# Attention contexts on GpSimd taken three heads at a time, with the value columns reordered

## The reference, cut to what matters

```python
a = cumsum(poids); b = cumsum(poids * Z); result = a * Z - b      # along the sorted axis
context = result for poids = v - mean(v)
sum_relu = result for poids = 1
norm = maximum(2 * sum_relu - (Z * total_v - total_vz), 1e-4)
context = 2 * context / norm
x = x + context
```

## Time and profile before

| | |
|---|---|
| median of 3 runs | 1457.23 us (1455.3 to 1460.18) |
| profiled execution | 1457.44 us, its span 1456.1 us |
| busy in the span | PE 1106.8, PEld 905.9, DVE 947.5, ACT 825.8, POOL 607.7 us |
| sign tiles on ScalarE (L1274) | 224, 430.7 us busy |
| sign tiles on VectorE (L1448) | 288, 395.5 us busy |
| head matmuls (L1161) | 8192, 389.8 us busy |
| sums on VectorE (L1459) | 32, 59.1 us busy |
| contexts on GpSimd (L1488 to L1496) | 224 operations, 290.0 us busy |

### The profile page before, as it was taken

How to read it: one execution, slowest core, us unless ns; L and a number is a source line. 1 busy time by engine, 2 the same in 40 slices (tenths; PEclk the granted TensorE clock), 3 DMA queues, 4 the chain that set the end, 5 groups by cost and what they waited for, 6 DMA issues and landing times. The chain is left out here.

```text
span 1456.1 us, 30443 instructions
## 1 busy us (share of the span) xinstructions
PE 1106.8 (76%) x12280; PEld 905.9 (62%) x12280; DVE 947.5 (65%) x1573; ACT 825.8 (57%) x961; POOL 607.7 (42%) x599
## 2 busy tenths in 40 slices
PE   5355689888989899979898896374638965974698
PEld 2143575478888897648888883153317963642697
DVE  4212656799999965589999995223834645764365
ACT  6211444699999933389999986222613325653233
POOL 3744001026666640105666663754172430227244
PEclk9778699999999999999999998787868987987799
DMA  8867300412212100012121203275233333003343
GB/s 245 296 206 230 111 1 1 179 45 81 84 65 89 60 1 1 5 58 88 61 88 60 89 32 102 102 225 184 74 129 91 121 118 97 1 1 132 88 118 102
DMA packets 84588, 140.61 MB, mean 97 GB/s; under 512 B 10574, under 2 KB 71246, under 8 KB 79950
## 3 DMA queue, kind: packets, MB, share of 16 engines
q1 hardware_dynamic: 70276, 102.15, 21.9%
q0 software_dynamic: 13056, 35.87, 6.9%
q10 hardware_dynamic: 1120, 0.66, 0.2%
HBM read 86.62 MB, written 56.27 MB: 98 GB/s over the span
## 5 line engine op out<-in xcount | busy, mean ns | idle before, releaser
L1274 ACT ACTIVATE b_signs<-b_q_everywhere,normed 128x2048 bf16<-128x2048 f32 x224 | 430.7, 1991 | 27.4 <-PE banks L1161 26.6
L1161 PE MATMUL banks<-b_value_parts,b_signs 128*128 128x102 bf16 x8192 | 389.8, 208 | 47.5 <-DVE b_signs L1448 46.7
L1161 PEld LDWEIGHTS banks<-b_value_parts,b_signs 128*128 128x128 bf16 x8192 | 375.7, 97 | 64.4 <-DVE b_signs L1448 47.1
L1448 DVE TENSOR_SCALAR b_signs<-b_q_everywhere,normed 128x2048 bf16<-128x2048 f32 x288 | 395.5, 1434 | 5.8 <-PE banks L1161 5.8
L569 POOL DMA_INDIRECT moe_slots<-normed,slot_of_token x128 | 124.6, 973 | 39.3 <-issue 33.8
L1488 POOL TENSOR_TENSOR normed<-b_sums,normed 128x16 f32<-128x16 f32 x32 | 35.2, 1099 | 222.1 <-DVE b_sums L1459 222.1
L382 PE MATMUL banks<-identity,normed 128*128 128x128 f32 x256 | 49.8, 328 | 57.1 <-ACT normed L358 57.1
L331 DVE BATCH_NORM_STATS2 ln_stats<-residual 128x6 f32<-128x256 f32 x192 | 71.1, 417 | 22.3 <-SPq L1689 10.5
L382 PEld LDWEIGHTS banks<-identity,normed 128*128 128x128 f32 x256 | 32.4, 163 | 66.3 <-ACT normed L358 52.5
L1476 POOL MEMSET b_value_parts<- 128x256 bf16 x2 | 2.7, 1334 | 169.1 <-PE banks L1035 169.1
L391 PE MATMUL banks<-normed_T,wg 128*8 128x256 f32 x256 | 71.7, 406 | 0.0
(11 more groups left out here) (281 smaller groups left out, 2458.2 us busy)
## 6 DMA issues: line engine op xcount, KB each, us to landing
b_q_everywhere<-q_rows SPq DMA_DIRECT2D x32, 1024.0 KB, 4.7
normed<-expert_rows SPq DMA_DIRECT2D x6, 1024.0 KB, 10.3
d_rows<-moe_slots SPq DMA_DIRECT2D x40, 129.5 KB, 2.2
f_rows<-moe_slots SPq DMA_DIRECT2D x40, 129.5 KB, 2.3
moe_slots<-a_empty SPq DMA_DIRECT2D x8, 518.0 KB, 10.0
a_rows<-moe_slots SPq DMA_DIRECT2D x16, 259.0 KB, 4.2
moe_empty_slots<-a_empty SPq DMA_DIRECT2D x8, 518.0 KB, 5.6
moe_slots<-moe_empty_slots SPq DMA_DIRECT2D x1, 4144.0 KB
```

What stands on the lines that cost most here:

```text
L1161: ins = nc.tensor.matmul(banks[qt // QPB][:, qt % QPB * VP:(qt % QPB + 1) * VP], t.SG[:, (hh * TB + kt) % RING, qt * P:(qt + 1) * P], t.VO ...
L1274: nc.scalar.activation(t.SG[:, g % RING, :], t.QB[:, hh % 2, :], ACT.Sign, bias=t.NKT[:, kt, hh % H:hh % H + 1]).then_inc(s.sign_a, 1)
L1448: nc.vector.tensor_scalar(t.SG[:, g % RING, :], t.QB[:, hh % 2, :], t.KTM[:, kt, hh % H:hh % H + 1], 2.0, ALU.is_gt, ALU.mult).then_inc(s. ...
```

## The change

The six groups of heads of a batch are (0..2), (3..5), (6..8), (9..11), (12..14) and (15). `dve_sum` is still done once a head, now into one of two buffers of three heads. `pool_context` runs once a group, after the last sum of it, with four operations: q times the first 17 columns, minus the second 17, times the reciprocal of the norm, plus the residual. `dve_norm` runs once a group behind the sign tile kt = 14 of the head that follows the group, and does the clip as well as the reciprocal. The columns of a part are now value, one, value times k, k, so that norm and values stand in one operand of 17 columns each. The buffers of sums and contexts move into the place of the batch's transposed x.

```diff
+TOGETHER = ((0, 3), (3, 6), (6, 9), (9, 12), (12, 15), (15, 16))
+GH = 3
+def group_of(h):
+    return next(i for i, (lo, hi) in enumerate(TOGETHER) if lo <= h < hi)
...
 def value_columns(t, p, product, part):
-    at = part * VC + (DH if product else 0)
+    at = part * VC + (DH + 1 if product else 0)
...
 def pe_held(k, batch):
-    for tiles, lo, hi, ones in ((ACT_KT, 0, 2 * DH, k.ONESB), (DVE_KT, 2 * DH, VC, k.MINUSB)):
+    split = lambda ap, lo, hi: ap.rearrange("p h (m e) -> p h m e", e=DH + 1)[:, :, :, lo:hi]
+    for tiles, lo, hi, ones in ((ACT_KT, 0, DH, k.ONESB), (DVE_KT, DH, DH + 1, k.MINUSB)):
...
-                if h and kt == 14:
-                    dve_norm(k, hh - 1)
+                if kt == 14 and h in [hi for lo, hi in TOGETHER]:
+                    dve_norm(k, batch, group_of(h - 1))
...
 def dve_sum(k, hh):
     nc.vector.wait_ge(s.acc, TB * (hh + 1))
-    if hh >= 2:
-        nc.vector.wait_ge(s.ctx, hh - 1)
-    nc.vector.tensor_reduce(t.A[:, hh % 2, :, :].rearrange("p (b i) c -> p b i c", i=QPB), parts, AX_X, ALU.add).then_inc(s.sum, 1)
+    if h == TOGETHER[group][0] and g >= 2:
+        nc.vector.wait_ge(s.ctx, g - 1)
+    nc.vector.tensor_reduce(t.A[:, g % 2, h - TOGETHER[group][0], :, :].rearrange("p (b i) c -> p b i c", i=QPB), parts, AX_X,
+                            ALU.add).then_inc(s.sum, 1)
...
-def dve_norm(k, hh):
-    nc.vector.wait_ge(s.nf, hh + 1)
-    nc.vector.reciprocal(t.N1[:, r, :], t.N2[:, r, :]).then_inc(s.n2, 1)
+def dve_norm(k, batch, group):
+    nc.vector.wait_ge(s.nf, batch * len(TOGETHER) + group + 1)
+    k.vs.step(nc.vector.tensor_scalar(t.N[:, 0:n, :], t.CT[:, 0:n, :, DH], NORM_MIN, None, ALU.max))
+    nc.vector.reciprocal(t.N[:, 0:n, :], t.N[:, 0:n, :]).then_inc(s.n2, 1)
...
-def pool_context(k, batch, h):
-    nc.gpsimd.wait_ge(s.sum, hh + 1)
-    step(nc.gpsimd.tensor_tensor(t.N1[:, r, :], t.A[:, r, :, 2 * DH], q, ALU.mult))
-    step(nc.gpsimd.tensor_tensor(t.N2[:, r, :], t.N1[:, r, :], t.A[:, r, :, 2 * DH + 1], ALU.subtract))
-    nc.gpsimd.tensor_scalar(t.N2[:, r, :], t.N2[:, r, :], NORM_MIN, None, ALU.max).then_inc(s.nf, 1)
-    step(nc.gpsimd.tensor_tensor(t.CT, t.A[:, r, :, 0:DH], q.unsqueeze(2).broadcast_to([P, TB, DH]), ALU.mult))
-    step(nc.gpsimd.tensor_tensor(t.CT, t.CT, t.A[:, r, :, DH:2 * DH], ALU.subtract))
-    nc.gpsimd.wait_ge(s.n2, hh + 1)
-    step(nc.gpsimd.tensor_tensor(t.CT, t.CT, t.N1[:, r, :].unsqueeze(2).broadcast_to([P, TB, DH]), ALU.mult))
-    nc.gpsimd.tensor_tensor(x, x, t.CT, ALU.add).then_inc(s.ctx, 1)
+def pool_context(k, batch, group):
+    nc.gpsimd.wait_ge(s.sum, batch * H + hi)
+    step(nc.gpsimd.tensor_tensor(ct, total[:, :, :, 0:DH + 1], every(t.QTM[:, :, lo:hi].rearrange("p t h -> p h t"), DH + 1), ALU.mult))
+    nc.gpsimd.tensor_tensor(ct, ct, total[:, :, :, DH + 1:VC], ALU.subtract).then_inc(s.nf, 1)
+    nc.gpsimd.wait_ge(s.n2, g + 1)
+    step(nc.gpsimd.tensor_tensor(ct[:, :, :, 0:DH], ct[:, :, :, 0:DH], every(t.N[:, 0:n, :], DH), ALU.mult))
+    nc.gpsimd.tensor_tensor(x, x, ct[:, :, :, 0:DH], ALU.add).then_inc(s.ctx, 1)
```

More of the change, by code:

```diff
@@ L233, in plan_attention @@
     at += 3 * TB * H
[L234 to L237, removed]
+    t.N = xn[:, at:at + GH * TB].rearrange("p (h t) -> p h t", h=GH)
+    at += GH * TB
+    done = 2 * GH * TB * VC
+    t.A = xn[:, 0:done].rearrange("p (r h t c) -> p r h t c", r=2, h=GH, t=TB)
+    t.CT = xn[:, done:done + GH * TB * (DH + 1)].rearrange("p (h t d) -> p h t d", h=GH, t=TB)
+    assert done + GH * TB * (DH + 1) <= KD * S
     t.ROW = xn[:, at:at + 2 * D].rearrange("p (s d) -> p s d", s=2)
@@ L268, in plan_attention @@
     t.Z = t.QB[0:H, :, :]
-    t.A = m.take("sums", [P, 2, TB, VC])
-    t.BQK = [t.A[:, 0, :, :].rearrange("p t c -> p (t c)")[:, 0:2 * D].rearrange("p (s d) -> p s d", s=2), bqk1]
+    t.BQK = [m.take("bqk", [P, 2, D])[:, :, :], bqk1]
     t.W = {n: m.take(n, [P, KD, D])[:, :, :] for n in ("wq", "wk", "wv")}
@@ L327, in dve_statistics @@
             elif stage == "route1":
-                nc.vector.wait_ge(s.ctx, B * H)
+                nc.vector.wait_ge(s.ctx, B * len(TOGETHER))
             elif stage == "route3":
@@ L1123, in pe_held @@
     nc.tensor.wait_ge(s.qtm, batch + 1)
-    for tiles, lo, hi, ones in ((ACT_KT, 0, 2 * DH, k.ONESB), (DVE_KT, 2 * DH, VC, k.MINUSB)):
+    split = lambda ap, lo, hi: ap.rearrange("p h (m e) -> p h m e", e=DH + 1)[:, :, :, lo:hi]
+    for tiles, lo, hi, ones in ((ACT_KT, 0, DH, k.ONESB), (DVE_KT, DH, DH + 1, k.MINUSB)):
         for tile in tiles:
             for b in range(4):
-                parts = lambda ap: ap.rearrange("p h (n c) -> p h n c", n=3)[:, :, :, lo:hi]
-                ins = nc.tensor.matmul(parts(k.bank[4 + b][:, 0:4 * VP].rearrange("p (h c) -> p h c", h=4)), ones[:, :],
-                                       parts(t.VOP[:, tile, 4 * b:4 * b + 4, :]), start=(tile == ACT_KT[0]), stop=(tile == DVE_KT[-1]))
+                ins = nc.tensor.matmul(split(k.bank[4 + b][:, 0:4 * VP].rearrange("p (h c) -> p h c", h=4), lo, hi), ones[:, :],
+                                       split(t.VOP[:, tile, 4 * b:4 * b + 4, :], lo, hi),
+                                       start=(tile == ACT_KT[0]), stop=(tile == DVE_KT[-1]))
     ins.then_inc(s.held_mm, 1)
@@ L1299, in dve_attention @@
                     dve_sum(k, hh - 1)
-                if h and kt == 14:
-                    dve_norm(k, hh - 1)
+                if kt == 14 and h in [hi for lo, hi in TOGETHER]:
+                    dve_norm(k, batch, group_of(h - 1))
         dve_sum(k, batch * H + H - 1)
-        dve_norm(k, batch * H + H - 1)
+        dve_norm(k, batch, group_of(H - 1))
 def dve_prepare(k, batch):
@@ L1362, in dve_prepare @@
     if batch:
-        nc.vector.wait_ge(s.ctx, batch * H)
+        nc.vector.wait_ge(s.ctx, batch * len(TOGETHER))
     nc.vector.wait_ge(s.zkt, batch + 1)
@@ L1454, in dve_sum @@
     nc, s, t = k.nc, k.s, k.at
+    batch, h = divmod(hh, H)
+    group = group_of(h)
+    g = batch * len(TOGETHER) + group
     parts = k.half[hh % 2][:, :, 0:QPB * VP].rearrange("p b (i n c) -> p b i c n", i=QPB, n=3)
     nc.vector.wait_ge(s.acc, TB * (hh + 1))
-    if hh >= 2:
-        nc.vector.wait_ge(s.ctx, hh - 1)
-    nc.vector.tensor_reduce(t.A[:, hh % 2, :, :].rearrange("p (b i) c -> p b i c", i=QPB), parts, AX_X, ALU.add).then_inc(s.sum, 1)
-def dve_norm(k, hh):
+    if h == TOGETHER[group][0] and g >= 2:
[3 more added lines that the diff above has]
+def dve_norm(k, batch, group):
     nc, s, t = k.nc, k.s, k.at
-    r = hh % 2
-    nc.vector.wait_ge(s.nf, hh + 1)
-    nc.vector.reciprocal(t.N1[:, r, :], t.N2[:, r, :]).then_inc(s.n2, 1)
+    n = TOGETHER[group][1] - TOGETHER[group][0]
+    nc.vector.wait_ge(s.nf, batch * len(TOGETHER) + group + 1)
+    k.vs.step(nc.vector.tensor_scalar(t.N[:, 0:n, :], t.CT[:, 0:n, :, DH], NORM_MIN, None, ALU.max))
+    nc.vector.reciprocal(t.N[:, 0:n, :], t.N[:, 0:n, :]).then_inc(s.n2, 1)
 def pool_attention(k):
@@ new lines, in pool_attention @@
+        nc.gpsimd.memset(t.VOP[:, :, :, DH], 1.0)
+        nc.gpsimd.memset(t.VOP[:, :, :, VC + DH], 0.0)
+        nc.gpsimd.memset(t.VOP[:, :, :, 2 * VC + DH], 0.0).then_inc(s.ones_set, 1)
+        for group in range(len(TOGETHER)):
+            pool_context(k, batch, group)
+def pool_context(k, batch, group):
+    nc, s, t, step = k.nc, k.s, k.at, k.ps.step
+    lo, hi = TOGETHER[group]
+    n, g = hi - lo, batch * len(TOGETHER) + group
+    total, ct = t.A[:, g % 2, 0:n, :, :], t.CT[:, 0:n, :, :]
+    every = lambda ap, c: ap.unsqueeze(3).broadcast_to([P, n, TB, c])
+    nc.gpsimd.wait_ge(s.sum, batch * H + hi)
[3 more added lines that the diff above has]
+    step(nc.gpsimd.tensor_tensor(ct[:, :, :, 0:DH], ct[:, :, :, 0:DH], every(t.N[:, 0:n, :], DH), ALU.mult))
+    x = k.X[:, batch * TB:(batch + 1) * TB, lo * DH:hi * DH].rearrange("p t (h d) -> p h t d", h=n)
+    nc.gpsimd.tensor_tensor(x, x, ct[:, :, :, 0:DH], ALU.add).then_inc(s.ctx, 1)
+    nc.gpsimd.wait_ge(s.ctx, g + 1)
```

9 lines of the change are left out of this document (removed).

## The result

The changed kernel takes 1468.6 us (median of 7 runs, 1465.92 to 1474.72) against 1456.12 us for the kernel before (median of 7, 1450.43 to 1460.18): a ratio of 1.0094 with a 95% interval of 1.0067 to 1.0121. It is slower by 9.8 to 17.6 us; 1473 was forecast. The profiled execution took 1468.6 us with a span of 1467.2, where before it was 1457.44 and 1456.1.

The account below looks back on a forecast made before the run. VectorE was taken to bound the head loops, until ScalarE's 13.25 us a head. Terms 3.7 + 1.6 + 1.4 + 1.2 = 7.9 us a batch, 15.8 for two, on 1457.44 give 1473 us; range 1457 to 1491.

Parts of the forecast that it names:

- VectorE pays for elements, the first quarter microsecond is free: Head loops: a GpSimd operation holds VectorE's signs up for its lone duration less 0.25 us.
- The rival that counted instructions: Each GpSimd instruction holds VectorE up for all its lone time, so fewer pay: 1433 us, chance 0.13.
- The price of a column: GpSimd's longer operations: 2.08 ns taken for each added column, between 1.78 and 2.36 ns.
- the hold-ups: VectorE's signs blocked by GpSimd: 24.0 us a batch before, 27.7 after, so +3.7, from +0.8 to +6.4.
- signs of being right: Held-up signs of 2.7 to 2.9 us, lone GpSimd operations of 1.7 to 1.85, periods about 19, 12.6 and 12.6.
- The rival of cheaper columns: Long GpSimd operations at 1.4 ns a column; blocks of about 19.8 us a batch pay for the rest: 1457, chance 0.11.
- Norm: Clip and reciprocal on VectorE: 2.7 us a batch in place of 1.1, so +1.6, from +0.4 to +3.4.
- Uneven load: Blocks fall in one of three head periods; ScalarE paces quiet heads: +1.4 and +1.2 us a batch.
- ScalarE's full pace in every quiet head: Rival: ScalarE's lead runs out, each quiet head pays 0.72 us, 5.8 a batch in place of 1.2: 1482, chance 0.13.
- Odd columns, taken at nothing: Product parts written from an odd bf16 column: 0 taken, at most 3.1 us a batch for ScalarE's operations.
- `pe_held`, taken at nothing: TensorE's held matmuls move as many columns in more pieces; doubling the 24-column ones adds about 1 us a batch: 0 taken.
- End of the batch: From the sum's end to the statistics after the second batch: 4.0 us before, 3.8 after; 0 taken, within 0.5.

Follow-up runs that it names:

- e2: The changed kernel with groups of one head, so four GpSimd operations a head with the columns unchanged; heads 14.50 us, loop 216.04 us against 218.30 in the change.
- e4: The changed kernel with six more GpSimd operations of 128x16 in each group of three heads; ratio 1.0080 to the kernel before.
- e3: The changed kernel with a group's four GpSimd operations cut to one column a tile, the rest of the contexts left out; loop 198.15 us.
- e6: The changed kernel with three operations of groups 0 to 3 each waiting for a VectorE sum, the norm moved later; loop 202.8 us, 15.5 less than the change.
- e7: The changed kernel with a ring of seven sign tiles in place of six; median 4.1 us below the change's, loop 216.76 us.
- e1: The kernel before with the new column order alone, contexts still one head at a time; +2.5 us, from near 0 to 4.8.
- e5: The kernel before with GpSimd's four 256-column operations of a head started with VectorE's sum two heads on; 1430.11 us, loops of 200.1 us.

## Why the prediction was right, step by step

*VectorE pays for elements, the first quarter microsecond is free.* Shown three ways: instructions taken out give nothing back (e2), instructions added cost nothing more (e4), columns taken out give back the whole hold-up (e3). The rival that counted instructions (1433) would have needed the opposite in e2 and e4, and longer signs than 1.286 us in e3. With the unblocked durations of e6 (1.66, 1.81, 1.50 and 1.68 us) and the forecast's 0.25, blocks of 1.41, 1.56, 1.25 and 1.43 us are due, and 1.41, 1.54, 1.24 and 1.44 were measured. The Trainium skill's rule (SBUF — State Buffer, "Who interferes with whom"), that the first to issue holds the shared ports for its whole instruction, agrees with these but for the first quarter of a microsecond.

*The price of a column is the term that was mis-sized.* 2.08 ns was taken; the four durations of e6 less those of the earlier trace rows, (6.65 - 2.66) us over 2144 columns, give 1.86, close to the lower end, 1.78, that the step from 16 to 256 columns gave. The mixer's 128x512, other operands on another line, was a poor neighbour. So a group costs 5.63 us where 6.13 were forecast, and the hold-ups moved by +1.25 us a batch in place of +3.7 (the prediction's own sum gives +1.5 at 1.86 ns). It is the largest error of the prediction. Two of its signs of being right missed their bounds for the same reason: the lone operations take 1.50 to 1.81 us (1.7 to 1.85 were named), the signs held up 2.52 to 2.83 (2.7 to 2.9). The rival of cheaper columns needed 1.4 ns.

*Norm.* +1.35 in place of +1.6. The clip (0.19 us) and the reciprocal (0.45 us) of 128x48 came about as forecast, with the sign behind them 0.52 us a time for 0.54; before it was 0.08.

*Uneven load.* Periods of 18.69, 12.64 and 13.02 us stood against 19, 12.6 and 12.6. The second quiet head carries the loss, as ScalarE's lead is used up by then; e7 shows the cause. The idle time is 2.2 us a batch against 1.4 + 1.2, and it divides otherwise: 0.64 in the second and third head of a batch, where ScalarE's full pace, 1.4, was forecast, and 1.66 in the quiet heads behind loaded ones, against 1.2. With the signs that run out ahead of these sums the uneven load costs 3.05, not 2.6. ScalarE's full pace in every quiet head (1482) is out.

*Odd columns, taken at nothing.* The prediction named value parts of over 0.7 us as a sign against itself, and they take 0.729. The term was right all the same and the sign badly chosen: the 0.056 us an operation do not reach the heads (e1).

*`pe_held`, taken at nothing, cost 1.25 us a batch.* The matmuls of the held part, in before and in the change, TensorE's timeline:

```profile
642.37 4.71 PE L1129 MATMUL banks<-b_value_parts,ones_bf 128*128 128x384 bf16 x28 [1.23 <-ACT b_value_parts L1251]
646.92 1.06 PE L1129 MATMUL banks<-b_value_parts,minus_ones_bf 128*128 128x24 bf16 x36
```

```profile
648.29 5.20 PE L1137 MATMUL banks<-b_value_parts,ones_bf 128*128 128x384 bf16 x28 [1.29 <-ACT b_value_parts L1260]
653.32 1.84 PE L1137 MATMUL banks<-b_value_parts,minus_ones_bf 128*128 128x24 bf16 x36
```

Both kinds became slower for the same columns: the 28 long ones take 4.55 us up to the first short one and then 5.03, the 36 short ones 1.06 and then 1.84, together 1.26 us more. The prediction had nearly that size beside it, for the short ones alone ("doubling them adds about 1 us a batch"), and took 0 without a reason. VectorE pays in full: its first sign of the batch waits there for TensorE, 2.88 us before and 4.15 after.

```profile
648.74 1.29 DVE L1448 TENSOR_SCALAR b_signs<-b_q_everywhere,normed 128x2048 bf16<-128x2048 f32 x1 [2.88 <-PE banks L1161]
```

```profile
655.92 1.28 DVE L1457 TENSOR_SCALAR b_signs<-b_q_everywhere,normed 128x2048 bf16<-128x2048 f32 x1 [4.15 <-PE banks L1170]
```

In e1 TensorE's held matmuls stand as far apart as in the change, and its +2.5 us is the 2 x 1.25 that this predicts. From the first held matmul to the first sum pass 20.19 us in both batches of before and of e5, and 21.45 in both of e1 and of the change. From the last sum of batch 0 to the first of batch 1 nothing of it shows (135.49 us before, 135.44 after), because the profiled execution of before had lost about as much by itself ahead of the held matmuls, the 115.30 us against 113.77 in e5 told above, though the work there is the same. From 559.8 to 562.1 us its granted clock was 0.50, the lower level (1.2 GHz), after 28.7 us of matmuls without a break and 1.8 us of pauses, and 128x512 matmuls took longer than in the change's at 1.00 (2.4 GHz):

```profile
561.21 0.63 PE L1048 MATMUL banks<-b_q_or_k_T,b_hidden_weights 128*128 128x512 f32 x1
```

```profile
567.45 0.40 PE L1056 MATMUL banks<-b_q_or_k_T,b_hidden_weights 128*128 128x512 f32 x1
```

The profiled execution of e7 has the low clock at the same place and 115.42 us; in the others it comes some 70 us later. Why it fell just there stays open; no run here was made for it.

*End of the batch.* From the last sum's start to the statistics it was 5.89 us and is 5.46 (forecast: 0 within 0.5). VectorE in the change, of before:

```profile
888.04 1.86 DVE L1471 TENSOR_REDUCE normed<-banks 128x544 f32<-128x1632 f32 x1 [1.43 <-PE banks L1170]
...
893.50 0.75 DVE L339 BATCH_NORM_STATS2 ln_stats<-residual 128x6 f32<-128x256 f32 x2 [1.49 <-POOL residual L1510]
```

Together, a batch: the hold-ups came out 2.45 us below the forecast and the norm 0.25, the uneven load 0.45 above it and `pe_held` 1.26; so 7.0 us in place of 7.9, and 14 for two batches, where 15.8 were forecast. The ratio gives 13.7, the medians 12.5. The mechanism held, but that the sum comes so near is in part luck: the hold-ups, whose growth was forecast at three times its size, stood against `pe_held`, which was left out.

## What to carry to other kernels

Before shortening an engine's work beside a busier one, work out which part of it the busier one pays for: here columns, not instructions, so a change that made 4 instructions of 21 (three heads) and left nearly all of the columns could not gain. Where work must stay, look for an instruction of the busy engine that does not mind it, and put the work beside that; the waits that do this were worth 2%, more than twice what the regrouping cost. Load spread evenly over the periods keeps the second engine's lead; the same load in every third period spends it.

## What the runs showed of the hardware

- GpSimd beside VectorE's reduction out of PSUM costs neither: 128x256 takes 0.65 us, as alone (0.641), and beside it or 128x816 (1.66 us) the reduction keeps its 1.84 to 1.86 us (e5, e6).
- 36 bf16 matmuls of 128x24 whose columns lie singly take 1.84 us, in pairs 1.06; 28 of 128x384 in runs of 16 columns 5.03 us, in runs of 32 4.55. The Trainium skill (PSUM — Partial Sum Buffer, "Specifications (TRN2)") says that any access to PSUM that isn't contiguous slows matmuls, and gives no price; in the trace shorter pieces are slower, which fits it, but inputs and outputs changed together here, so which of them costs isn't shown.
- An odd start of 16-element bf16 runs costs a 128x512 write of ScalarE 0.056 us (e1).
